# The low part of tiles 4 and 5 as two operations, tile 5's behind the additions of step 1

## The reference

```python
    q = q * cos + _rotate_half(q) * sin
    k = k * cos + _rotate_half(k) * sin
    scores = jnp.einsum('bhtd,bhsd->bhts', q, k) * (1.0 / np.sqrt(HD))
    scores = jnp.where(mask, scores, -jnp.inf)
    att = jax.nn.softmax(scores, axis=-1)
    out = jnp.einsum('bhts,bhsd->bhtd', att, v)
...
    x = _layernorm(x + _L0_attn_ref(x, ...), axis=-1)
    x = _layernorm(x + _L0_ffn_ref(x, ...), axis=-1)
```

## Time and profile before

| | |
|---|---|
| median of three runs | 1170.01 us (1169.91 to 5764.48) |
| the profiled execution, its own time | 1172.84 us |
| its span, first to last instruction | 1171.0 us |
| TensorE busy, in the span | 1119.6 us, granted clock 0.991 of full speed |
| VectorE, ScalarE, GpSimd busy | 802.8, 620.2, 820.7 us |
| attention, heads 1 to 31 | about 60 to 910 us |
| feed-forward part | about 930 to 1171 us |

### The profile page before, as it was taken

One profiled execution on the slowest core, in us unless ns is written; L12 is line 12 of the kernel. 1 busy time (PEld: TensorE's weight loads), 2 busy tenths in 40 slices (PEclk: granted clock), 3 DMA queues, 4 the chain that ended last, 5 costly groups with the idle time before them and its releaser, 6 DMA issues.

```text
span 1171.0 us, 18940 instructions
## 1 busy us (share of the span) xinstructions
PE 1119.6 (96%) x5346; PEld 942.4 (80%) x5346; DVE 802.8 (69%) x1416; ACT 620.2 (53%) x1122; POOL 820.7 (70%) x543
## 2 busy tenths in 40 slices
PE   7799999999999999999999999999997799999997
PEld 6678888887888788878888887888775588888885
DVE  5688788778777887788788877777888742222224
ACT  4556666666666566565666566666654342212224
POOL 3489978996898789789978996898774343333431
PEclk9899999999999999999999999999999899999999
DMA  5766555555554666466555655555455301111101
GB/s 187 190 154 154 141 139 136 151 125 142 134 145 124 146 159 157 120 153 158 150 129 147 152 125 135 149 143 125 126 139 134 106 19 53 54 54 54 54 0 72
DMA packets 148346, 144.56 MB, mean 123 GB/s; under 512 B 15200, under 2 KB 128864, under 8 KB 148320
## 3 DMA queue, kind: packets, MB, share of 16 engines
q1 hardware_dynamic: 136160, 124.31, 41.3%
q10 hardware_dynamic: 12160, 19.93, 6.2%
HBM read 37.23 MB, written 2.10 MB: 34 GB/s over the span
## 4 chain that ended last, share of the span: by engine, by line
PE 62%; POOL 16%; issue 10%; DMA 4%; DVE 3%; ACT 2%; SPq 1%; ACTq 0%; POOLq 0%; DVEq 0%
PE ACC L1064 13%; PE ACC L1066 13%; PE ACC L1065 13%; PE S L1064 4%; PE S L1066 4%; PE S L1065 4%; POOL PT_lo L499 4%; POOL qk_raw L473 4%; PE S L1080 3%; PE S L1082 3%; PE S L1081 3%; POOL rope_s L474 3%; POOL Q_lo L483 2%; DMA rope_s<-qk_raw 2%; POOL wq_lo L453 2%
## 5 line engine op out<-in xcount | busy, mean ns | idle before, releaser
L803 DVE CUSTOM_DVE_ANT_0 S<-S,mask 128x128 f32<-128x128 f32 (+7 forms) x256 | 194.4, 759 | 155.0 <-PE S L1082 155.0
L593 ACT ACTIVATE probs<-S,neg_max 128x128 f32<-128x128 f32 (+7 forms) x256 | 189.2, 739 | 207.4 <-DVE neg_max L803 204.9
L499 POOL TENSOR_TENSOR PT_lo<-PT_lo,PT_hi 128x896 fp32r<-128x896 f32 (+1 forms) x97 | 218.3, 2250 | 36.2 <-ACT PT_hi L600 36.1
L814 DVE STREAM_TRANSPOSE turned<-probs 128x128 f32<-128x128 f32 (+7 forms) x256 | 197.8, 773 | 4.0 <-ACT probs L593 4.0
L874 DVE SCALAR_TENSOR_TENSOR y<-ACC,row_rcp,y 128x512 f32<-128x512 f32 x256 | 177.2, 731 | 16.6 <-PE ACC L1066 16.6
L473 POOL TENSOR_TENSOR qk_raw<-qk_raw,cos_sb 128x512 f32<-128x512 f32 x76 | 116.9, 1538 | 97.2 <-DMA rope_s<-qk_raw 97.1
L600 ACT ACTIVATE PT_hi<-PT_lo 128x896 fp32r<-128x896 f32 (+3 forms) x160 | 162.3, 1015 | 29.6 <-DMA PT_lo<-turned 29.2
L551 POOL TENSOR_TENSOR PT_lo<-rope_s,PT_hi 128x512 fp32r<-128x512 f32 x28 | 36.3, 1297 | 156.9 <-ACT PT_hi L742 156.9
L1064 PE MATMUL ACC<-PT_hi,V_hi 128*128 128x512 f32 (+3 forms) x384 | 134.2, 349 | 7.0 <-DVE PT_lo L821 4.4
L1080 PE MATMUL S<-K_hi,Q_hi 128*128 (+5 forms) x384 | 133.3, 347 | 7.4 <-ACT probs L593 5.0
L1065 PE MATMUL ACC<-PT_lo,V_hi 128*128 128x512 f32 (+3 forms) x384 | 134.9, 351 | 0.0
(11 more groups left out here) (129 smaller groups left out, 2552.0 us busy)
## 6 DMA issues: line engine op xcount, KB each, us to landing
PT_lo<-turned SPq DMA_DIRECT2D x256, 112.0 KB, 2.5
PT_lo<-turned SPq DMA_DIRECT2D x128, 208.0 KB, 4.0
rope_s<-qk_raw ACTq DMA_DIRECT2D x152, 128.0 KB, 3.8
PT_lo<-turned SPq DMA_DIRECT2D x128, 128.0 KB, 2.6
PT_lo<-turned SPq DMA_DIRECT2D x128, 80.0 KB, 2.3
wq_raw<-in_L_attn_wq_dram SPq DMA_DIRECT2D x32, 256.0 KB, 3.0
wo_raw<-in_L_attn_wo_dram SPq DMA_DIRECT2D x32, 256.0 KB, 3.7
turned<-in_L_ffn_gate_w_t_dram SPq DMA_DIRECT2D x7, 512.0 KB, 3.9
```

The lines of the kernel that those rows point to most:

```text
L499: nc.gpsimd.tensor_tensor(lo, lo.bitcast(F32), hi.bitcast(F32), ALU.subtract).then_inc(pt_lo_done[half], 1)
L593: nc.scalar.activation(dst, src, ACT.Exp, bias=neg_max[:, at:at + 1], scale=-1.0, accum_out=row_sum[:, j % 2, i:i + 1]).then_inc(exp_done, 1)
L803: nc.vector.tensor_tensor_reduce(src, src, bias, scale=1.0, scalar=MASKED, op0=ALU.add, op1=ALU.min, accum_out=neg_max[:, at:at + 1]).then ...
L814: nc.vector.transpose(dst.rearrange("p b (r i) -> p r b i", i=QB), src.rearrange("p (r b i) -> p r b i", b=4, i=QB)).then_inc(turn_done, 1)
```

## The change

On VectorE `pt_low` takes a tile and no longer a group. `LOW_AT` names tile 4 in step 0 and tile 7 in step 2, and the low part of tile 5 is made in step 1, behind the two additions of that step. Tile 4 now has 640 elements and tile 5 has 768. TensorE waits for four counts a head of `pt_lo_done[1]` where it waited for three. Behind the last head GpSimd takes tiles 4 and 5 one by one too.

```diff
-        "head": REP, "pt0": REP * 2, "pt1": REP * 3,
+        "head": REP, "pt0": REP * 2, "pt1": REP * 3, "lo1": REP * 4,
...
-LOW_AT = {0: (2,), 2: (4,)}
+LOW_AT = {0: (4,), 2: (7,)}
...
-            for k in (2, 3):
-                pt_low(k)
+            for tiles in (SENT[2][:1], SENT[2][1:], SENT[3]):
+                pt_low(2 + (tiles == SENT[3]), tiles)
...
-            def pt_low(k):
-
-                dve.wait_ge(pt_hi_done[1], n["pt1"] + (k - 1))
-                lo, hi = of_tiles(PT_lo, SENT[k]), of_tiles(PT_hi, SENT[k])
+            def pt_low(t):
+
+                dve.wait_ge(pt_hi_done[1], n["pt1"] + {4: 1, 5: 1, 7: 3}[t])
+                lo, hi = of_tiles(PT_lo, (t,)), of_tiles(PT_hi, (t,))
                 nc.vector.tensor_tensor(lo, lo.bitcast(F32), hi.bitcast(F32), ALU.subtract).then_inc(pt_lo_done[1], 1)
-                n.add("pt1", 3 * (k == 4))
+                n.add("pt1", 3 * (t == 7))
...
-                for k in LOW_AT.get(i, ()) if j > 0 else ():
-                    pt_low(k)
+                for t in LOW_AT.get(i, ()) if j > 0 else ():
+                    pt_low(t)
                 for t in row_tiles(j, i):
                     add_rows(t, j - 1)
+                if i == 1 and j > 0:
+                    pt_low(5)
...
-            pt_low(4)
+            pt_low(7)
...
-                            pe.wait_ge(pt_lo_done[half], (n[f"pv{half}"] + 1) * (2 + half))
+                            pe.wait_ge(pt_lo_done[half], (n[f"pv{half}"] + 1) * (4 if half else 2))
```

More of the change, by code:

```diff
@@ L492, in qk_halves, with pt_low @@
                 return [k_half(a, k_slot, half) for a in (K_hi, K_lo)]
-            def pt_low(k):
+            def pt_low(k, tiles=None):
                 half = SENT[k][0] // HT
                 pool.wait_ge(pt_hi_done[half], n[f"pt{half}"] + (k - 1 if half else 1))
-                lo, hi = of_tiles(PT_lo, SENT[k]), of_tiles(PT_hi, SENT[k])
+                lo, hi = [of_tiles(pt, tiles or SENT[k]) for pt in (PT_lo, PT_hi)]
                 nc.gpsimd.tensor_tensor(lo, lo.bitcast(F32), hi.bitcast(F32), ALU.subtract).then_inc(pt_lo_done[half], 1)
```

## The result

The changed kernel takes 1192.4 us in the median of four runs (1191.15 to 1196.85). The kernel before, run beside it, takes 1170.1 us. The ratio over the runs, without the one of 5764 us among those of the kernel before, is 1.0197, 95% interval 1.0181 to 1.0214 (the two medians alone give 1.019). The kernel is slower, by about 2.0%; whether by more than 2% these runs do not tell, since the interval lies on both sides. The forecast was 1186 us, with a range from 1167 to 1195.

A forecast was written before the change was run, and what follows sets the result against it. TensorE, busy 1119.6 of 1171.0 us, was held in tight heads last by tile 7's low part. Tight heads 11.6 plus other heads 4.6 gave +16 us: 1189 profiled, 1186 as median (2.8 lower), range 1167 to 1195.

The forecast's parts named there:

- The lock: VectorE operation with two SBUF inputs waits until GpSimd's operation ends; for tile 5's low part in step 1, some 1.1 us.
- The lag: In step 1, tile 5's low part is asked for 0.13 us behind the start of GpSimd's `Q_lo`.
- tight heads: Ten heads without K or V projection between tile 3's scores and output rows of tiles 2 and 3; 11.6 us lost.
- the first pattern: Nine tight heads in the order of the rows at 389 to 397: 1.0 us lost each, 9.0 together.
- the second collision: In three tight heads tile 7's later request falls behind GpSimd's next operation (L473): some 0.9 us more, 2.8 together.
- The tenth: Tight head at 57.60, where VectorE goes first and tile 7 already waited for `Q_lo`: 0.2 us won.
- The other heads: Outside the tight heads, nine with 0.90 to 0.22 us of room before the product lose 4.6 us, the rest nothing.
- The 0.1 us a head: VectorE's low parts of tiles 4 and 5: 1408 elements computed in place of 1536, saving 0.1 us a head.
- The first: Rival: in step 1 VectorE gets in ahead of `Q_lo`; 1169 us, not slower than before; chance 0.2.
- The second: Rival: in all ten tight heads tile 7's request also falls behind a GpSimd operation; +27 us, 1197; chance 0.12.
- The third: Rival: the additions come earlier, the 12.8 us of waits go, nothing else is late; 1157 us; chance 0.05.
- the ties at 255.73 and 443.08: VectorE and GpSimd start within some hundredths: at 255.73 VectorE took 2.39 us, at 443.08 it went first in 1.73.

The follow-up runs named there:

- five new orders: The changed kernel and four variants placing VectorE's low parts differently (split at step 0, between the additions, unsplit behind them, ahead of tile 7's): 1192.4, 1222.5, 1178.3, 1187.2, 1183.2 us.
- the split at step 0: Against the kernel before: tiles 4 and 5 each in an operation of its own, both in step 0, without the move; 1222.5 us, ratio 1.0435.
- the one-input run: Changed kernel with tile 5's subtraction on VectorE replaced by a block transpose with one SBUF input, same place and waits; 1169.9 us, ratio 0.9991 to the kernel before.

## Why the prediction was right

**What bounds the kernel.** Right. The waits for `y` shrank by 9.6 us and nothing came of it, because tile 7's low part was the later one. I had said 6 us would be left; it is 3.2.

**The lock.** Right, and shown by taking the second input away. The lag came out at 0.10 to 0.13 us in the tight heads, against 0.13 forecast, and the operation at 1964 ns against "about 2.0". By the rule of the Trainium skill, page SBUF — State Buffer, section Who interferes with whom, a VectorE instruction with one SBUF input, outside the modes in which it uses two ports, stays clear of GpSimd; the transpose beside `Q_lo` agrees with that, at 964 ns.

**The heads.** From the starts of the product of half 1 in both traces the loss by the last head is 18.4 us. The nine tight heads of the first pattern lost 0.7 to 1.5 us each, 8.8 together, where I had 11.8: the term that was mis-sized is the second collision, put at 2.8. The requests for tile 7 met no L473 in most of them, since the whole head had moved and L473 started 0.3 to 0.9 us behind them. The tenth, at 57.60, lost 1.3 where I had a gain of 0.2: it no longer had its old alignment (a 640-element row of 1.74 us at 57.51). The other heads lost 8.2 us, of which 3.1 are the clock's (below); the remaining 5.1 stand against 4.6. So the right total comes in part from errors that cancel: the second collision was 2.8 too much, the tenth head 1.5 too little. (The 0.1 us a head that the shorter operations were to save is 0.05 by the prediction's own figures, 1.73 less 0.77 and 0.91.)

**What I had not reckoned with.** The clock: two heads with a half-speed stretch in them took 28.9 and 29.1 us from product to product (402.50 to 431.44, 740.11 to 769.24), four at the same place of their groups without one 27.4 to 27.7. That is some 1.55 us each, 3.1 together, and it agrees with the 1.54 to 1.6 us of the whole operation behind the additions. So 18 us of span are 15 of lock and 3 of clock, against 16 of lock. The profiled execution came out at 1191.15 us, 2 above the 1189 of the sum; the prediction's sum has no term for the clock. The median of the runs lies 1.2 us above the profiled one, where I had put it 2.8 below: 4 us more. These two are what the forecast of 1186 fell short by. The slower runs have a lower mean clock (0.988, 0.986 and 0.981, against 0.991 in the profiled one); that the clock makes them slower is likely and not shown, as there is no trace of them.

**The rivals.** The first (VectorE goes ahead of `Q_lo`) happened in two of 31 heads, at 116.41 and 145.79, where tile 6's low part was late and the operation waited for that instead (2.03 and 1.50 us); in the 29 others it waited for `Q_lo`. That it did not happen in more hangs on a tenth of a microsecond: with GpSimd's work begun earlier it does in 14. So the mechanism was right, and that the lag kept its sign was in part luck: the prediction gave the other outcome a chance of 0.2. The second (tile 7 collides as well) shows in two of the ten tight heads, at 64.31 (1.84 us for tile 7's low part, where it took 2.18 before) and at 852.96 (1.39 us). The third is what the changed kernel's diff suggests and what its profile refutes. What decided the ties at 255.73 and 443.08 in the kernel before, some hundredths of a microsecond, stays open.

## What to carry to other kernels

Before cutting an operation in two, find in a profile who holds what two engines share, and at what time: each part queues for it anew, and its wait lasts until the other engine's operation ends, whatever the part's own length (here 1.1 us for an operation of 0.9). When several results are due at one place, follow each of them and move the latest; a wait that a profile shows may hide two others right behind it. Where two engines race, starting the other engine's chain earlier can be worth more than a new order of one's own: here it gave 1159.7 us, and none of the five new orders came below 1178.

## What was not expected of the hardware

TensorE's granted clock, from 60 to 900 us, and TensorE's gaps ahead of each fall. In the kernel before the longest gaps are 2.1 and 1.8 us (at 883.59 and 887.72), and the clock never fell. In the changed kernel there are six gaps of 1.8 us, and it fell to its lower level, 1.2 GHz, behind two of them; behind those of 2.5, 2.2 and 2.0 us at 66, 854 and 882 us it did not. In the kernel with the whole operation behind the additions it fell behind four of five gaps of 1.84 to 1.93 us. In the same kernel it fell behind a gap of 2.6 and not behind one of 2.8. In the split at step 0 it fell behind all eight gaps of 3.0 to 3.6 us. And in the one-input run it fell behind one of 1.42 us (a row of TensorE, and one of the view by windows):

```profile
65.01 0.54 PE L1071 MATMUL ACC<-PT_hi,V_hi 128*128 128x512 f32 x1 [1.42 <-DVE PT_lo L826]
...
65.00:69.00 4.00, 3.99 (x11) 3.14 (x12) 2.64 (x5) 1.89 (x5) 3.92 (x4) 0.57 0.02 4
```

So the length of the last gap alone does not tell whether the clock falls, and what does stays open here. One such stretch lasts 3.4 us or twice that, and one of 3.4 us costs some 1.55 us where it could be read off. The changed kernel's four runs spread over 5.7 us, and the slowest has the lowest mean clock.
